# Storing the first group of a resident ring batch by batch: a conditioned residual on one core

## What is computed

```python
def _L0_cond_ref(x, condition, weights):
    W = weights[condition]
    return jnp.einsum('bct,bcd->bdt', x, W)
x = x + _L0_cond_ref(x, itok_B_0_15, L0_cond_weights)
```

## Time and profile before

| what | before |
|---|---|
| median of three executions | 319.93 us |
| the profiled execution's own time | 319.72 us |
| its span, first to last instruction | 318.0 us |
| TensorE matmuls busy | 250.7 us (79%) |
| VectorE busy | 146.8 us (46%) |
| DMA moved | 135.29 MB, mean 425 GB/s |
| one load or store of a group | 4096 KB in the page's list of DMA issues |
| granted TensorE clock, mean | 0.899 of full speed |

### The profile page before, as it was taken

One profiled execution on the slowest core, in us unless ns is written; L12 is line 12 of the kernel. 1 busy time (PEld: TensorE's weight loads), 2 busy tenths in 40 slices (PEclk: granted clock), 3 DMA queues, 4 the chain that ended last, 5 costly groups with the idle time before them and its releaser, 6 DMA issues.

```text
span 318.0 us, 1353 instructions
## 1 busy us (share of the span) xinstructions
PE 250.7 (79%) x512; PEld 106.6 (34%) x512; DVE 146.8 (46%) x65; POOL 18.9 (6%) x69
## 2 busy tenths in 40 slices
PE   0099999992896959959698695988959599695980
PEld 0044444440342424324243342433414244242430
DVE  0026676674074552525537174272725517355261
POOL 0001000000000010100100000000000100000000
PEclk9999999997597997969989797797989969799795
DMA  8999999999999999999999999999999999999997
GB/s 330 396 462 408 387 458 420 437 439 416 458 400 462 408 449 433 425 458 400 462 404 453 429 429 453 404 458 408 449 429 429 458 404 458 408 449 429 429 409 325
DMA packets 5323, 135.29 MB, mean 425 GB/s; under 512 B 586, under 2 KB 714, under 8 KB 842
## 3 DMA queue, kind: packets, MB, share of 16 engines
q1 hardware_dynamic: 2584, 68.29, 50.2%
q10 hardware_dynamic: 2738, 66.98, 48.9%
HBM read 68.16 MB, written 67.11 MB: 425 GB/s over the span
## 4 chain that ended last, share of the span: by engine, by line
DMA 61%; PE 33%; DVE 3%; issue 0%; SPq 0%
PE product L101 33%; DMA x_ring<-x 31%; DMA out<-x_ring 30%; DVE x_ring L117 3%; SPq L58 0%
## 5 line engine op out<-in xcount | busy, mean ns | idle before, releaser
L101 PE MATMUL product<-x_ring,chosen_weights 128*128 128x512 f32 x512 | 250.7, 654 | 58.5 <-DMA x_ring<-x 58.5
L117 DVE TENSOR_TENSOR x_ring<-product,x_ring 128x2048 f32<-128x2048 f32 x64 | 146.7, 2291 | 162.7 <-PE product L101 162.7
L101 PEld LDWEIGHTS product<-x_ring,chosen_weights 128*128 128x128 f32 x512 | 106.6, 211 | 201.8 <-issue 125.0
L89 POOL COPY chosen_weights<-weight_table 128x128 f32 x64 | 18.7, 293 | 285.9 <-DVE x_ring L117 278.9
L111 DVE TENSOR_SCALAR state_row<-condition_row 1x64 int32<-1x64 int32 x1 | 0.2, 182 | 2.0 <-DMA condition_row<-condition 2.0
L149 POOL MEMSET const-float32-0.0<- 128x1 f32 x1 | 0.1, 98 | 0.1
L149 POOL MEMSET const-bfloat16-1.0<- 128x1 bf16 x1 | 0.1, 101 | 0.0
L149 POOL MEMSET const-uint8-127<- 128x1 uint8 x1 | 0.1, 101 | 0.0
L149 POOL MEMSET const-float32-1.0<- 128x1 f32 x1 | 0.1, 98 | 0.0
L149 POOL BASE_LOAD x1 | 0.0, 12 | 0.1
## 6 DMA issues: line engine op xcount, KB each, us to landing
x_ring<-x SPq DMA_DIRECT2D x16, 4096.0 KB, 28.7
out<-x_ring ACTq DMA_DIRECT2D x15, 4096.0 KB, 29.5
out<-x_ring ACTq DMA_DIRECT2D x3, 1024.0 KB
weight_table<-weights SPq DMA_DIRECT2D x1, 1024.0 KB, 4.9
out<-x_ring ACTq DMA_DIRECT2D x1, 896.0 KB
out<-x_ring SPq DMA_DIRECT2D x1, 124.0 KB
condition_row<-condition ACTq DMA_DIRECT2D x1, 0.2 KB
out<-x_ring SPq DMA_DIRECT2D x1, 4.0 KB
```

Of the source, the lines that this page charges most:

```text
L89: pool.tensor_copy(chosen_weights[b][:, :], weight_table[:, bass.ds(state[b] * features, features)]).then_inc(weights_chosen[b], 1)
L101: last = pe.matmul(product[:, b % psum_slots, m * BANK_COLUMNS:(m + 1) * BANK_COLUMNS], chosen_weights[b][:, :], x_ring[:, bass.ds(b * tim ...
L117: dve.tensor_tensor(tile, product[:, b % psum_slots, :], tile, AluOpType.add).then_inc(sum_done[b], 1)
```

## The change

Group 0 is no longer stored as a whole. ACT waits for each of its four batches' sums in turn and issues a store of that batch's 8 KB of each row. The loop over whole groups starts at group 1. As four stores now count up the semaphore of room 0 by 64 in place of 16, SP's wait ahead of each load into room 0, and ACT's last wait, take 48 counts more: a new helper gives the count.

```diff
+        def stores_wanted(times, room):
+            return 16 * (times + (GROUP - 1 if room == 0 else 0))
+
...
                 if g >= ROOMS:
-                    sp.wait_ge(room_stored[room], 16 * (g // ROOMS))
+                    sp.wait_ge(room_stored[room], stores_wanted(g // ROOMS, room))
...
-            for g in range(groups - 1):
+
+            for i in range(GROUP):
+                act.wait_ge(sum_done[i], sums_wanted(0, i))
+                act.dma_start(out[0, :, i * time:(i + 1) * time], x_ring[:, i * time:(i + 1) * time]
+                              ).then_inc(room_stored[0], 16)
+            for g in range(1, groups - 1):
...
-                act.wait_ge(room_stored[r], 16 * (groups // ROOMS + (GROUP + 1 if r == room else 0)))
+                act.wait_ge(room_stored[r], stores_wanted(groups // ROOMS, r)
+                            + (16 * (GROUP + 1) if r == room else 0))
```

## The result

The changed kernel takes 320.42 us, the median of 22 executions, against 319.94 for the kernel before, also of 22. The ratio is 1.002, with a 95% interval of 1.0011 to 1.0029: slower by half a microsecond in the medians and by 0.35 to 0.93 us in the interval. That is small but clear of zero, and it lies on the line of 0.2% up to which the prediction speaks of no change. The profiled execution took 320.76 us with a span of 319.0.

The account below looks back on a forecast made before the run. The prediction took the DMA engines, 99.1% taken, as the bound. Its terms gave 319.72 + 0 + 0 + 0.2 + 0 = 319.9 us for the profiled execution, 0.2 under the median, hence 320.1; range 319.2 to 321.0.

Parts of the forecast that it names:

- That nothing would be gained: Stores of group 0: the DMA engines have no idle stretch for earlier stores to fill; earlier issue priced at 0.
- the loss that I had added to load 2: Landing of load 2: 0.9 us added for the dip in DMA speed after the first store's issue.
- Turns by packet: Load and store queues alternate packet by packet, not by bytes; stores get about 20% of the engines, load 4 at 55.2.
- The first store's own loss: The 0.9 us dip at 36 to 40 us moves to about 26 to 30 at equal cost: 0, bounds -0.9 to +2.7.
- Smaller packets: Group 0's stores in 8 KB rows: 424 GB/s instead of 433 for 4.19 MB, +0.2 us, lower end 0.
- rival A: Each of the four small stores disturbs the engines as the first store did: +2.7 + 0.2, or 322.8 us; chance 6%.
- All later issues as before: After load 4, issued at 55.2 +/- 0.5 us, all later issues should stand where they stood.
- The end: After the last sum at 311.52 us, leftover work keeps engines at 424 GB/s to 314 and 378 to 316 us.
- A fixed price for each DMA: The Trainium skill's fixed cost, about 2.0 us per DMA, would make three more DMAs +6 us; the prediction doubted it.

Follow-up runs that it names:

- kernel with late quarters: The changed kernel, but all four stores of group 0 wait for the group's last sum: 320.45 us against 319.95 for the kernel before, ratio 1.0014.
- fifteenfold run: Every group from 0 to 14 stored by four DMAs of 8 KB rows after its last sum: 327.78 us against 320.00 for the kernel before.
- pair with the light TensorE: Kernel before and changed kernel, both multiplying only 512 of 2048 columns per batch, batch added to itself, product left out: 319.76 and 320.04 us.

## Why the prediction was right, and where it was off

**That nothing would be gained: right, for the reason given.** The engines had no hole that the earlier stores could fill. The predicted landings were 37.0 for load 2, 49.1 for load 3 and an issue of load 4 at 55.2; measured were 37.1, 49.2 and 54.74. The kernel with late quarters shows it by experiment, too: 320.45 without the earlier issue, 320.42 to 320.51 with it. The close landings owe something to luck: the sums of groups 0 and 1 came one us earlier in this execution than in the trace that I had worked from, and the loss that I had added to load 2 was 0.4 us and not 0.9.

**Turns by packet: right.** 176 against 166 data packets from 30 to 46 us, and load 4 not before 52 us. The rows from which I took it, 1 KB packets on a few engines, were thin, but read rightly.

**The first store's own loss: moved, but not as a whole.** The dip lies at 26 to 30 us, as forecast, but costs 0.4 us there and not 0.9. The term was 0 for the pair of them; the runs show half a microsecond less here and 0.5 to 1.0 more in 55 to 75 us, which the prediction had nowhere.

**Smaller packets: the term that was too small.** I put it at +0.2 us from the spacing of 8 KB packets on one queue, with 0 as the lower end and no upper end. All in all a group costs 0.5: the fifteenfold run gives 0.52, the changed kernel 0.48. The forecast of 320.1 was 0.3 short of 320.42 for this, inside its range. The rows that I used, the end of the kernel, have one busy queue and no handover, so they could only show the smaller part. The row that bore on the rest stood in the prediction, as the first store's dip, but I took it as a matter of the first store after an empty queue on the stores' side. It goes with a handover between queues, and with all groups in quarters there are more of them: the loads' queue runs dry when it gets four fifths of the time. This is rival A's mechanism in another place, and at about a tenth of its price (+0.3 beyond the spacing, where A had +2.7).

**All later issues as before: not quite.** Load 4 lands after 25.4 us in both, but load 5 is issued at 72.64 and not at about 71, since store 1 ends later; the loads then land sooner after their issue (a median of 26.9 us, not 28.7) and the stores later (32.1, not 29.5). The two queues keep another phase, and the end shows it in different rows, not in the load of the engines.

**The end.** I had called it safe with full engines behind the last sum. In the profiled execution it was not fully so (0.92 in 312 to 314 us), but moving the last sum by a us in the kernel before cost 0.1 in the medians (its interval reaches 0.5). How much of the half microsecond is slow packets and how much is the sixteen engines ending apart stays open. In the two profiled pages the queues took 99.1% of 318.0 us and 98.9% of 319.0, 0.4 us more work; the other 0.6 of the longer span is engines without work. The pair with the light TensorE, 0.28 apart, is too coarse to divide it.

**A fixed price for each DMA: not here.** Four DMAs with 32 KB packets cost 0.08 us in all, inside the error, and the +6 us are far outside it. By the Trainium skill, page "DMA: Bandwidth & Descriptors", section "Anatomy of one DMA", which tells of DMAs issued by GpSimd, the fixed part is mostly the wait for the completion. By that reading it would cost only someone who waits; in this kernel only SP waits, and once for all four quarters.

## What to carry to other kernels

When the DMA engines are full, an earlier store was worth nothing here: add up what must be moved before the transfer that waits for it, and see whether anything is left out. Before splitting a transfer, look at what becomes of its rows: a split along the row makes the packets smaller, and queues that take turns by packet then share unevenly, fall out of step and, in the traces here, pay when one comes in beside the other; a split that keeps rows whole and spreads them over the partitions cost nothing that could be measured. And price a split in the steady state by doing it to every group: half a microsecond for one is hard to measure, eight for fifteen is not.

## What the runs showed of the hardware

- Stores of rows from 32 neighbouring partitions are slow. With group 0 stored as four DMAs of 32 whole neighbouring rows the kernel took 325.93 us, 5.98 more. In 51 to 58 us, when only that queue was at work, the DMA view of this kernel shows

```profile
DMA packets 64, 1.41 MB, mean 201 GB/s; under 512 B 21, under 2 KB 21, under 8 KB 21
q10 hardware_dynamic: 64, 1.41, 94.7%
```

  under half of 433 GB/s with sixteen busy engines. With every fourth row in each DMA the same queue has, in 50 to 55 us,

```profile
DMA packets 100, 2.16 MB, mean 433 GB/s; under 512 B 34, under 2 KB 34, under 8 KB 34
```

  and the kernel 320.08 us. By the Trainium skill, page "SBUF — State Buffer", section "Door 1: The DMA port swizzle", what counts is how many of 16 SBUF ports the partitions reach, and 32 neighbours reach only half of them. The trace agrees, with 201 against 433 GB/s. The two kernels also differ in where a DMA's rows lie in `out`, and no run here parts this from the partitions.
- The granted clock of the last group differs between executions and hardly moves the time. Its 32 matmuls took 15.71 us before, with 0.88 granted in 297 to 301 us, 17.07 in the changed kernel with 0.70, and 13.75 with 1.00 where TensorE had been kept busy ahead of them. The medians of the kernels in which they ended at other times lie within a few tenths of their counterparts.
